# Pacing SyncE's slab loads and pad stores by their landings in a recurrent-attention and expert kernel

## What is computed

```python
x = _layernorm(x + attention(x))
scores = softmax(x @ gate_w + gate_b)
topk_s, topk_i = top_k(scores, 2)
wf = dispatch weights, zero where an expert is not picked
for i in range(8):
    wi = wf[:, i:i + 1]
    h = relu(xf * wi @ w1[i] + b1[i])
    y = h @ w2[i] + b2[i]
    out = where(wi > 0, y, out)
x = _layernorm(x + out)
```

## Time and profile before

| what | before |
|---|---|
| median of 3 runs without a profile | 451.95 us (451.29, 451.95, 452.58) |
| profiled execution, first to last instruction (its span) | 491.3 us |
| profiled execution, any other time of it | none shown |
| mean granted TensorE clock over the span | 0.934 |
| PE, DVE, ACT, POOL busy | 413.0, 369.9, 345.0, 325.3 us |
| slabs: SP, 71 loads | 258.0 KB each |
| pads: SP, 8 stores ahead of slot 18 and one early in the program | 65.0 KB each |

### The profile page before, as it was taken

The page is one execution under the profiler, slowest core; times in us unless marked ns, Lnnn a source line. Parts: engine busy times, 40 slices in busy tenths (PEclk is TensorE's granted clock), DMA queues, the critical chain, the costliest instruction groups (busy, mean ns, idle before and its releaser), DMA issues.

```text
span 491.3 us, 10567 instructions
## 1 busy us (share of the span) xinstructions
PE 413.0 (84%) x2806; PEld 324.4 (66%) x2806; DVE 369.9 (75%) x1216; ACT 345.0 (70%) x980; POOL 325.3 (66%) x298
## 2 busy tenths in 40 slices
PE   5988999988899879997999187495469899999994
PEld 4544555555555435784967187485469799999994
DVE  6489999999999976688688177664227677777874
ACT  2687999998899789979659245553426577777773
POOL 1077999999999976605555544444634567777775
PEclk9999999999999999999799775977759999999998
DMA  7177555657554525100111632434625667777720
GB/s 207 34 183 161 142 152 137 165 142 178 130 137 123 147 47 157 59 0 18 45 35 41 192 94 66 114 110 123 159 86 164 169 168 195 213 192 193 195 87 23
DMA packets 44378, 61.17 MB, mean 125 GB/s; under 512 B 6670, under 2 KB 29713, under 8 KB 42400
## 3 DMA queue, kind: packets, MB, share of 16 engines
q1 hardware_dynamic: 39712, 51.63, 41.2%
q0 software_dynamic: 4320, 8.47, 4.9%
q10 hardware_dynamic: 288, 0.41, 0.3%
HBM read 47.49 MB, written 13.44 MB: 124 GB/s over the span
## 4 chain that ended last, share of the span: by engine, by line
PE 42%; POOL 27%; issue 12%; another core or an unknown queue 6%; DVE 6%; ACT 5%; DMA 1%; POOLq 0%; SPq 0%; DVEq 0%; ACTq 0%
POOL states L2168 15%; PE bank L761 14%; PE bank L745 12%; PE bank L395 4%; POOL o_scale L2180 3%; POOL x_sb L2186 3%; POOL row_buffers L2159 3%; PE bank L371 2%; PE bank L751 2%; POOL slab L2174 2%; PE bank L408 2%; PE bank L384 2%; ACT row_buffers L461 1%; DVE x_sb L478 1%
## 5 line engine op out<-in xcount | busy, mean ns | idle before, releaser
L942 POOL DMA_INDIRECT out_rows<-h2t x71 | 70.6, 995 | 56.1 <-DVE h2t L909 28.2
L596 POOL DMA_INDIRECT expert_regions<-row_buffers,row_i x64 | 62.4, 975 | 68.5 <-DVE row_i L580 30.9
L761 PE MATMUL bank<-ew,h2t 128*128 x568 | 83.8, 294 | 14.6 <-DVE h2t L893 10.6
L761 PEld LDWEIGHTS bank<-ew,h2t 128*128 128x128 f32 x568 | 73.5, 202 | 19.1 <-issue 17.3
L745 PE MATMUL bank<-h2t,slab 128*128 128x128 f32 x568 | 82.3, 291 | 4.4 <-ACT h2t L779 3.4
L2168 POOL TENSOR_TENSOR states<-states,queries 128x1024 f32<-128x1024 f32 x32 | 75.2, 2371 | 6.0 <-DVE states L1906 5.9
L745 PEld LDWEIGHTS bank<-h2t,slab 128*128 128x128 f32 x568 | 74.7, 205 | 5.5 <-issue 5.1
L1906 DVE TENSOR_TENSOR_SCAN states<-bank,kv 128x512 f32<-128x512 f32 x64 | 72.9, 1202 | 0.7 <-ACT bank L1443 0.7
L786 ACT ACTIVATE h2t<-bank,slab 128x128 f32<-128x128 f32 x142 | 44.1, 365 | 24.6 <-PE bank L745 15.9
L884 DVE TENSOR_SCALAR h2t<-bank,slab 128x128 f32<-128x128 f32 x142 | 42.7, 342 | 13.2 <-remote 6.6
L779 ACT ACTIVATE h2t<-bank 128x128 f32<-128x128 f32 x71 | 19.7, 278 | 45.8 <-PE bank L751 17.3
(11 more groups left out here) (215 smaller groups left out, 914.6 us busy)
## 6 DMA issues: line engine op xcount, KB each, us to landing
slab<-in_slabs SPq DMA_DIRECT2D x71, 258.0 KB
kv<-values_by_head SPq DMA_DIRECT2D x30, 512.0 KB, 5.5
h2t<-expert_regions SPq DMA_DIRECT2D x71, 65.0 KB
x_sb<-in_x SPq DMA_DIRECT2D x32, 128.0 KB, 6.0
values_by_head<-row_buffers SPq DMA_DIRECT2D x15, 256.0 KB, 2.1
out_rows<-h2t POOLq DMA_INDIRECT x71
expert_regions<-row_buffers,row_i POOLq DMA_INDIRECT x64
expert_regions<-pad_record SPq DMA_DIRECT2D x9, 65.0 KB, 3.9
```

The source lines that it names most:

```text
L596: pool.indirect_dma_start(out=regions, out_offset=bass.IndirectOffsetOnAxis(ap=row_i[:, q, g:g + 1].bitcast(U32), axis=0), in_=rec[:, ring ...
L761: ins = pe.matmul(bank[7][:, 0:D], c_ht[:, s, c * P:(c + 1) * P], ew2[:, bass.ds(e * HC + c * D, D)], start=(c == 0), stop=(c == HC - 1 an ...
L942: pool.indirect_dma_start(out=out, out_offset=bass.IndirectOffsetOnAxis(ap=rc[:, q, D + 1:REC].bitcast(U32), axis=0), in_=c_y[:, item % RO ...
```

## The change

SP gets two kinds of waits. Among the first eight slabs, slab k (from 2 on) is held until slab k - 2 has landed, so that two are in flight. Among the eight pad stores, after the second, fourth and sixth SP waits until all pads issued so far have landed. Every engine issues the same instructions in the same order as before; SP has 426 of them in both programs. The lines behind the two edits move down by two and by four.

```diff
                     sp.dma_start(regions[bass.ds(pads[e % 4], P), :], pad_record[:, :]).then_inc(padded, 16)
+                    if e % 2 == 1 and e + 1 < E:
+                        sp.wait_ge(padded, 16 * (e + 1))
 
 
             sp.wait_ge(o_scaled, PAIRS)
...
             for k in range(SLABS_C):
                 if k % 2 == 0:
                     rows_and_firsts(k)
+                if k >= 2:
+                    sp.wait_ge(slab_ld[k - 2], 16)
                 bring_slab(k)
```

## The result

The changed kernel takes **456.40 us** (median of 4 runs, 454.98 to 457.28) beside 451.62 us for the kernel before (4 runs, 450.78 to 452.58): ratio 1.0109, 95% interval 1.0082 to 1.0135. It is 4.8 us slower; 452.0 was predicted, with 446 to 456 as the range.

The account below looks back on a forecast made before the run. The prediction took the last stage as PE-bound at full clock and the middle stage's stalls as belonging to the profiled execution. Slabs 0 plus pads 0 left the runs' median, 452.0 us, range 446 to 456.

Parts of the forecast that it names:

- The bookkeeping: Whole profiled execution: its 39.4 us over the timed runs match 29.6 to 40.5 us of middle-stage stalls, absent from runs.
- The first rival: Stalls by slabs and pads are partly real and pacing removes them: faster, 446.7 us, or 442.2 with both; chance 0.31.
- The slabs: SP's first eight slabs, two in flight: path cost 0 to 0.1 us, taken as 0.
- The cover named: Before the first records on SP: the wait for early scatters hides the slab pace, which otherwise costs 1.4 us.
- The pads: Three waits among SP's eight pad stores: 6.0 us on SP, bounds 4.5 to 9.9, path cost 0.
- the third rival: SP's slab and pad waits are already met when reached, so nothing is held: 452 us; chance 0.10.
- the slack of record 18: Spare time before ACT reads the record queued behind the pads on SP: 8.6 us, 3.3 at the steady pace.
- the 6.0 us fit in the slack: path cost 0: Pad waits on SP delay the record behind them less than its spare time: path cost 0, bounds 0 to 6.6 us.
- The time from SP's release to the reading: From ACT's slot 9 step freeing SP to ACT's reading of record 18: 28.5 us, 19.1 without two stalls.
- The landing: Time for record 18 to land after SP issues it: 2.1 us, subtracted in the spare-time estimate.
- The rival "Record 18 comes late": SP behind the pads: 6.0 us less 3.3 of spare time leaves 2.7 us, slower, 454.7 us; chance 0.26.

Follow-up runs that it names:

- experiment 0: The kernel before, unchanged, timed against itself and profiled a second time: 451.35 us, ratio 0.9994.
- experiment 1: The changed kernel's six slab waits added to the kernel before, without the pad pauses: 450.63 us, ratio 0.9997.

## Why the prediction was wrong

**The bookkeeping held.** The 39.4 us missing from the timed runs belonged to that one execution, its stalls and the lower clock behind them (granted 0.934 over the span, 0.969 in experiment 0): profiled again, the kernel spans 450.9 us. The prediction gave them to the recording, with the Trainium skill, "NOTIFIC — the notification-queue block", section 7.1, behind it. The runs leave that part open: the twelve later executions were recorded too, and their spans of 447.7 to 459.6 us have no room for such stalls. What delayed the first execution is not shown; it is shown that the kernel does not need that time. The first rival, that pacing would take stalls away, fell with it: no version here is faster than before.

**The slabs held.** Cost 0 was predicted, with a last issue between 278.5 and 281.8; it came at 281.27, and experiment 1 gives 0.9997. The cover named was the right one too: with the waits, SP still stands for the early scatters before the first record, 2.5 us in experiment 1 and 0.9 in the changed kernel, where experiment 0 has 8.4.

**The pads held on SP.** 6.0 us were predicted for three pauses, 2.6 a pair to land. The pads took 10.44 instead of 5.15 us, 5.3 more, with waits of 6.3 us; the third rival, waits already met when reached, fell.

**What failed is the slack of record 18**, and with it the step "the 6.0 us fit in the slack: path cost 0". The prediction had 8.6 us for an undisturbed run and 3.3 at a steady pace, and put the timed runs "between, nearer the first". Measured, it is 2.0 to 2.9, below both. Two terms of it were wrong:

- *The time from SP's release to the reading.* 28.5 us in the execution of the earlier trace rows, of which only the two stalls that the chain of waits named (9.4 us) were taken off: 19.1. In experiment 0 it is 13.3: DVE's half of slot 9, which frees slab 17, ends at 318.8, and ACT reads record 18 at 332.11. The other 5.8 us stand in no stall of the chain; where most of them stand is shown behind these points. The pace worked out from the same trace, 2.6 us a slot, has the same fault: from slot 9 (311.96) to slot 18 (332.11) ACT's readings in experiment 0 are 2.24 us apart.
- *The landing.* 2.1 us, from a median of other transfers. From issue to reading, where ACT waited for it, record 18 took 3.61 us in the changed kernel, 2.96 and 2.97 with the pauses alone, 2.91 with seven pauses; slab 18 is issued 0.54 us ahead of it. A record that leaves alone comes near the 2.1: record 0 of experiment 0, 9 us behind the last slab, took 1.95 us, and that of the changed kernel, 1.7 us behind it, 3.50. That the slab is the cause was not tested by itself.

By the measured terms: 13.3 - 7.9 (318.8 to the issue at 326.72) - 2.9 to 3.6 = 1.8 to 2.5 before ACT stands, and 0.4 more before PE does, since PE turns the record 0.44 us after ACT's 0.41 us reading is done. Against 5.3 of delay that leaves the wait of 2.93 us.

Where the 5.8 us that were not taken off stand can be read from the trace of before. One row for the stretch from SP's release to the reading before, one for it in experiment 0 (the clock is the number after POOL's column), and pieces of the chain that ended last before, from 341 to 370 us (start, us, what):

```profile
341.10:369.70 28.60, 16.86 (x99) 16.19 (x99) 9.49 (x37) 12.14 (x47) 12.70 (x13) 0.63 0.44 119
```

```profile
318.80:332.10 13.30, 12.82 (x113) 12.23 (x112) 9.57 (x37) 10.91 (x42) 10.26 (x11) 1.00 0.73 203
```

```profile
358.65 2.07 PE bank L761 x8
...
362.93 2.05 PE bank L745 x8
...
365.19 1.71 PE bank L761 x8
...
367.22 1.71 PE bank L745 x8
```

With a fifth of 1.79 us at 342.12, these groups take 9.3 us of the chain; five of them at the 0.90 to 1.15 each of experiment 0's chain would take 4.5 to 5.8. So some 4 of the 5.8 us are matmuls at the lower clock, on the path but not called a stall: taking off the two stalls left in what the matmuls lose behind them.

**The rival "Record 18 comes late" was the right mechanism**, with its place and its sign (ACT's nineteenth reading ends an idle stretch on the landing of a record). It priced the loss at 2.7 us, 454.7. The wait was about that size, 2.93, though partly by luck: the delay it started from (6.0) and the slack it took off (3.3) were both too large, and measured they are 5.3 and 2.2. What it lacked is the term behind the wait, 1.8 to 2.9 us that the matmuls lose at 1.2 GHz. The prediction had the lower clock before it, as a mean of 0.80 in the earlier trace rows, and used it only to argue about the stalls.

## What to carry to other kernels

Take the slack of a transfer from an execution whose span agrees with the timed runs. One that is 9% longer hides how tight the schedule is, and subtracting the stalls that have a name does not restore it, since here the slow matmuls behind the stalls stayed in; if no other exists, the lower of two estimates of slack is the one to plan with.

A pause on an issuing queue is paid by what stands behind it there. The same three pauses cost 4.8 to 6.2 us ahead of a record with 2 to 3 us to spare and 1.1 us, within what the runs can tell from nothing, three slots earlier. And a wait that reaches PE can be paid twice: here waits of 2.4 us and more brought the matmuls after them to the lower clock.

## What was not expected of the hardware

PE's granted clock fell after a short wait in an otherwise full stretch: after 2.93, 2.84, 2.42 and 2.09 us of idling two to three groups took 1.4 to 2.05 us each instead of 1.06 to 1.15; after 8.46 us it was two groups, no more than that; after 1.41 and 0.72 us none, with the clock at 1.00 throughout. The price did not grow with the wait (2.9 us behind 2.84, 2.1 behind 8.46): in the long wait the clock stood at 0.50 from 334 us on, while PE idled until 339.80, so that the greater part of the slow stretch held no matmuls.

The kernel before was recorded once at a span of 491.3 us and once at 450.9, the same program; register operations on SP of up to 710 ns marked the long one; the same line has at most 51 ns in experiment 0.
